# A decoder layer's attention: the softmax denominators summed from a GpSimd pre-addition, after the value passes

## What is computed

```python
scores = jnp.einsum('bhsd,bhtd->bhst', q, k)
scores = (scores + alibi[None]) / math.sqrt(D_HEAD)
scores = 30.0 * jnp.tanh(scores / 30.0)
scores = jnp.where(causal[None, None], scores, -jnp.inf)
probs = jax.nn.softmax(scores, axis=-1)
ctx = jnp.einsum('bhst,bhtd->bhsd', probs, v)
ctx = ctx.transpose(0, 2, 1, 3).reshape(N, S, N_HEADS * D_HEAD)
return ctx @ Wo + bo
```

## Time and profile before

| | us |
|---|---|
| median of 3 runs | 1212.09 (1209.39 to 1213.41) |
| span of the profiled execution, first to last instruction | 1209.9 |
| its own time | not listed apart from the three runs above |
| TensorE busy | 1179.2 (97% of the span) |
| VectorE / GpSimd / ScalarE busy | 862.2 / 583.5 / 531.2 |

### The profile page before, as it was taken

One profiled execution on the slowest core, in us unless ns is written; L12 is line 12 of the kernel. 1 busy time (PEld: TensorE's weight loads), 2 busy tenths in 40 slices (PEclk: granted clock), 3 DMA queues, 4 the chain that ended last, 5 costly groups with the idle time before them and its releaser, 6 DMA issues.

```text
span 1209.9 us, 24907 instructions
## 1 busy us (share of the span) xinstructions
PE 1179.2 (97%) x9875; PEld 816.0 (67%) x9890; DVE 862.2 (71%) x1286; ACT 531.2 (44%) x598; POOL 583.5 (48%) x493
## 2 busy tenths in 40 slices
PE   4989999999999999999999999999999999999998
PEld 3656557656657566576565677777886786786784
DVE  6787978777877777688787588889653653654554
ACT  6676664654655645637556400000342432432341
POOL 0445454644645546445456399998332322322221
PEclk9989999999999999999999999999999999999999
DMA  9463352544335425434355367771000000000000
GB/s 325 136 199 117 118 160 70 161 157 118 116 126 169 132 89 168 162 103 131 108 170 168 128 129 151 147 143 50 1 1 18 1 19 18 0 17 18 1 18 35
DMA packets 128126, 124.04 MB, mean 103 GB/s; under 512 B 31612, under 2 KB 89346, under 8 KB 128066
## 3 DMA queue, kind: packets, MB, share of 16 engines
q1 hardware_dynamic: 103112, 117.00, 31.6%
q10 hardware_dynamic: 24960, 6.29, 3.2%
HBM read 81.76 MB, written 35.21 MB: 97 GB/s over the span
## 4 chain that ended last, share of the span: by engine, by line
PE 89%; DVE 4%; ACT 2%; DMA 2%; POOL 1%; issue 1%; SPq 1%; POOLq 0%; DVEq 0%; ACTq 0%
PE bank L885 12%; PE bank L641 11%; PE bank L642 10%; PE bank L643 10%; PE bank L961 9%; PE bank L962 9%; PE bank L717 6%; PE bank L984 5%; PE bank L983 4%; PE bank L706 3%; PE bank L707 3%; PE bank L719 3%; DMA unit_halves<-halves 1%; PE bank L649 1%; ACT region_c L1098 1%
## 5 line engine op out<-in xcount | busy, mean ns | idle before, releaser
L1877 POOL TENSOR_TENSOR parts<-parts 128x512 f32<-128x512 f32 x80 | 130.3, 1632 | 118.0 <-DVE parts L1353 118.0
L641 PE MATMUL bank<-hT_hi,w_hi 128*128 128x256 f16 x640 | 175.7, 274 | 4.8 <-DVE hT_lo L1337 4.8
L642 PE MATMUL bank<-hT_lo,w_hi 128*128 128x256 f16 x640 | 175.4, 274 | 0.0
L643 PE MATMUL bank<-hT_hi,w_lo 128*128 128x256 f16 x640 | 175.3, 274 | 0.0
L1882 POOL TENSOR_SCALAR_AFFINE_SELECT region_c<-region_c 128x512 f32<-128x512 f32 x128 | 106.9, 859 | 135.6 <-ACT region_c L1101 135.5
L885 PE MATMUL bank<-kv,toep 128*128 128x288 f32 (+2 forms) x660 | 157.8, 401 | 0.7 <-ACT qT L1134 0.5
L885 PEld LDWEIGHTS bank<-kv,toep 128*128 128x128 f32 x660 | 123.7, 190 | 34.0 <-ACT qT L1134 0.7
L1098 ACT ACTIVATE region_c<-bank,cap_scale 128x1536 f32<-128x1536 f32 x64 | 98.7, 1542 | 94.2 <-PE bank L707 93.7
L1888 POOL TENSOR_TENSOR ctx_lo<-ctx,ctx_hi 128x512 f16<-128x512 f32 x64 | 89.0, 1392 | 83.4 <-ACT ctx_hi L1077 83.4
L2011 POOL TENSOR_TENSOR sqsum<-sqsum,toep 128x512 f32<-128x512 f32 x56 | 71.1, 1269 | 110.1 <-ACT toep L1263 110.0
L961 PE MATMUL bank<-odd_hi,guT 128*128 128x256 f16 x512 | 112.4, 273 | 0.0
(11 more groups left out here) (177 smaller groups left out, 2638.6 us busy)
## 6 DMA issues: line engine op xcount, KB each, us to landing
unit_halves<-halves SPq DMA_DIRECT2D x80, 256.0 KB, 2.2
q_both<-unit_halves SPq DMA_DIRECT2D x64, 256.0 KB, 2.9
q_high<-unit_halves SPq DMA_DIRECT2D x64, 128.0 KB, 3.0
toep<-kernel_padded SPq DMA_DIRECT2D x32, 256.0 KB, 4.1
wffn<-w_gu SPq DMA_DIRECT2D x6, 1280.0 KB, 6.2
cpair<-ctx_pairs SPq DMA_DIRECT2D x32, 176.0 KB, 4.7
xin<-x SPq DMA_DIRECT2D x8, 512.0 KB, 3.7
region_o<-wq SPq DMA_DIRECT2D x4, 1024.0 KB, 11.2
```

The source lines that it names most:

```text
L641: pe.matmul(dst, lh, rh, start=first and k == 0, stop=False)
L642: pe.matmul(dst, lh, rl, start=False, stop=False)
L643: mm = pe.matmul(dst, ll, rh, start=False, stop=last and k == n - 1)
L1877: pool.tensor_tensor(slot[:, 0], slot[:, 0], slot[:, 1], ALU.add).then_inc(unit_summed, 1)
```

## The change

GpSimd gets one more instruction per group, behind the two mask selects: it adds the second key tile's masked weights to the first tile's, for queries 128 to 255, into a new buffer of two slots. The sums become two sets of four 128-column products with ones: queries 0 to 127 from the first tile, queries 128 to 255 from the new buffer. They stand behind the two value passes, and wait for the addition. The addition waits for the masks, and from group 2 on for the sums of two groups before. ScalarE's wait for group 5's slot is now on the sums. `gsum` goes, to make room, and the thresholds' sums are kept in `gthr`.

```diff
--- before.py
+++ after.py
@@ -166,9 +166,9 @@
             dist_scale = sb1("dist_scale", [P, Q_PIECES])
             undo_o = sb1("undo_o", [P, 1])
             dcol = sb1("dcol", [HM, 1])
-            gsum = sb1("gsum", [P, WQT, 512 // GROUP])
+            gthr = sb1("gthr", [P, WQT, 512 // GROUP])
             gscale = sb1("gscale", [P, WQT, 512 // GROUP], BF16)
-            gthr = sb1("gthr", [P, WQT, 512 // GROUP])
+            key_sum = sb1("key_sum", [P, 2, REP, P])
 
             w_bf = sb1("w_bf", [P, WQT, 512], BF16)
             wffn = sb1("wffn", [P, WQT, 512])
@@ -316,6 +316,7 @@
         tanh_done = sem("tanh_done")
         exp_done = sem("exp_done")
         masked = sem("masked")
+        keys_added = sem("keys_added")
         pv_filled = sem("pv_filled")
         sums_filled = sem("sums_filled")
         rsum_turned = sem("rsum_turned")
@@ -724,9 +725,6 @@
                 if g == 0 and first:
                     pe.wait_ge(unit_turned, 6)
                     pe.wait_ge(wscale_step, SCALE_STEPS * I_Q[3] + 1)
-                if g or not first:
-                    pe.wait_ge(rsum_turned, NG * b + g)
-                weigh(bank[:, SUM_BANK, 0:S], g % 3, lambda t: sum_ones[:]).then_inc(sums_filled, 1)
                 if g == 0:
                     pe.wait_ge(v_ready, TT * (b + 1))
                 if g >= 2 or not first:
@@ -734,6 +732,14 @@
                 for v in range(2):
                     mm = weigh(bank[:, pv_bank(g), v * S:(v + 1) * S], g % 3, lambda t: value_half(t, g, v))
                 mm.then_inc(pv_filled, 1)
+                pe.wait_ge(keys_added, NG * b + g + 1)
+                if g or not first:
+                    pe.wait_ge(rsum_turned, NG * b + g)
+                for j in range(REP):
+                    mm = pe.matmul(bank[j * SQ:(j + 1) * SQ, SUM_BANK, 0:P], sum_ones[:], sc_first[:, g % 3, j, 0:P], start=True, stop=True)
+                for j in range(REP):
+                    mm = pe.matmul(bank[j * SQ:(j + 1) * SQ, SUM_BANK, P:S], sum_ones[:], key_sum[:, g % 2, j, :], start=True, stop=True)
+                mm.then_inc(sums_filled, 1)
 
             def output(b, g):
                 pe.wait_ge(ctx_lo_done, NG * b + g + 1)
@@ -1117,7 +1123,7 @@
                         high_unit(b, EARLY + step - 2)
                     if step == NG:
                         round_share(b)
-                act.wait_ge(pv_filled, NG * b + LAST_IN_CUT + 1)
+                act.wait_ge(sums_filled, NG * b + LAST_IN_CUT + 1)
                 for tiles in HALVES:
                     spread(b, gthr, w_cut, THRESHOLDS, tiles)
                 high_ctx(b, NG - 1, False)
@@ -1461,10 +1467,10 @@
             def find_thresholds(f):
                 base = QUANT_STEPS * f
                 dve.wait_ge(w_rounded, f + 1)
-                dve.tensor_reduce(gsum[:], w_bf[:].rearrange("p t (n c) -> p t n c", c=GROUP), AX_X, ALU.add,
+                dve.tensor_reduce(gthr[:], w_bf[:].rearrange("p t (n c) -> p t n c", c=GROUP), AX_X, ALU.add,
                                   apply_absolute_value=True).then_inc(quant_step, 1)
                 dve.wait_ge(quant_step, base + 1)
-                dve.tensor_scalar(gscale[:], gsum[:], 1.0 / GROUP, 1e-8, ALU.mult, ALU.max).then_inc(quant_step, 1)
+                dve.tensor_scalar(gscale[:], gthr[:], 1.0 / GROUP, 1e-8, ALU.mult, ALU.max).then_inc(quant_step, 1)
                 dve.wait_ge(quant_step, base + 2)
                 dve.tensor_scalar(gthr[:], gscale[:], 257.0 / 512.0, None, ALU.mult).then_inc(quant_step, 1)
                 dve.wait_ge(quant_step, base + 3)
@@ -1882,6 +1888,11 @@
                     last = pool.affine_select(s, s, pattern=[[0, REP], [1, P]],
                                               compare_op=ALU.is_ge, fill=0.0, base=0, channel_multiplier=-1)
                 last.then_inc(masked, 1)
+                n = NG * b + g + 1
+                pool.wait_ge(masked, n)
+                if g >= 2:
+                    pool.wait_ge(sums_filled, n - 2)
+                pool.tensor_tensor(key_sum[:, g % 2], sc_first[:, g % 3, :, P:S], sc_second[:, g % 3], ALU.add).then_inc(keys_added, 1)
 
             def low_ctx(b, g):
                 pool.wait_ge(ctx_hi_done, NG * b + g + 1)
```

## The result

The changed kernel takes **1234.34 us** (median of 4, 1232.58 to 1235.86) against 1212.59 of the kernel before (4 runs, 1209.39 to 1213.41): ratio **1.0181 [1.0168, 1.0194]**, slower by some 22 us. The forecast was 1227.3, in a range to 1236.

What follows compares the result with a forecast made beforehand. TensorE, 89% of the chain, was taken as the bound. Six loop batches of +2.5 us made +15.2, the ends -0.4 and +0.4: span 1209.9 to 1225.1, by the median 1227.3; range 1206 to 1236.

Steps and rivals of the forecast that it cites:

- Removed: In TensorE's sums, two 128-column halves take 0.22 instead of 0.45 us: 0.22 less a group, 1.76 a batch.
- That the halves don't save: Rival: the two 128-column halves take no less, as the second needs a switch; +14 on top, chance 0.02.
- The addition: One GpSimd addition of 128x512 float32 per group, behind the masks: 1.25 us plus 0.1 for its wait.
- The cheap addition: Rival: the GpSimd addition takes 0.6 us like a select; -6, 1206, faster, chance 0.12.
- Place 1: Step 7, next batch's normalisation: addition between mask and deviation, turn 1.35 later, TensorE waits 2 us; net +0.03 a batch.
- Place 3, output(0): Step 5: additions delay masks, parts and low_ctx(0), which ends about 323.1; TensorE waits about 0.9 us.
- Place 2, output(1): Step 6: VectorE's wide addition gets in before low_ctx(1), which output(1) needs; TensorE waits about 1.6 us.
- The exclusion: A VectorE instruction with two SBUF inputs and a GpSimd one reading SBUF exclude each other for the whole instruction.
- Only Place 1 counts: Rival: no wait at output(0) and (1), as VectorE's wide work finds another gap; -2, 1210, chance 0.16.
- The clock falls: Rival: TensorE's clock falls behind the turn's wait, from 1.3 us more idle time on; +29, 1241, chance 0.07.
- The ends: First batch -0.4 (bounds -1.8 and +1.8); last batch +0.4, from -1.8, +1.6 at output(1) and +0.6 at output(3).
- Costed at nothing (a): VectorE's chain of a group starts some 1.3 us later, behind the value passes; nothing, or 1.3 a batch if cover failed.

Runs made afterwards that it cites:

- experiment 3: Changed kernel without the addition, second half of the sums reading the second key tile alone, exponential's scale 0.01 instead of 30: 1204.37 us, 0.9936.
- experiment 6: Changed kernel with each addition one step later, before the next masks, and the deviation ahead of mask(7), in the last batch of mask(5): 1202.94 us, 0.9929.
- experiment 10: Kernel before with only the deviation ahead of mask(7) in the loop and of mask(5) in the last batch: 1211.0 us, 0.9991.
- experiment 4: Changed kernel with keep_x2 and the deviation ahead of addition 7 in step 7 of the loop: 1225.58 us, 1.0107.
- experiment 7: Changed kernel with VectorE's 3584-wide subtraction of step 4 cut to 8 elements: 1234.54 us, 1.0186.
- experiment 1: Changed kernel with the old sums (256 + 128 columns) and no addition, value passes still ahead of the sums: 1213.61 us, 1.0013.
- experiment 2: Changed kernel with its addition and waits, but the old sums of 256 + 128 columns: 1231.08 us, 1.0149.
- experiment 9: Changed kernel with every addition done twice in a row: 1299.23 us, 1.0736.
- experiment 5: Changed kernel with each addition one step later in GpSimd's queue, ahead of the next group's masks: 1213.34 us, 1.0013.
- experiment 11: Kernel of experiment 6 with the old sums in the old order and no additions in the first and last batch: 1201.14 us, 0.9912.

## Why the prediction was right, and where not

The forecast, slower, held, and in the main by its mechanism: the additions' places in GpSimd's queue cost more than the shorter sums give. A third of the loss (6.8 of 21.3) is the falling clock, which it had as a rival. By its own steps:

- **Removed.** 0.22 a group was 0.21, 1.70 a batch (experiment 3, and 6 against 10). That the halves don't save, a rival, falls.
- **The addition.** 1.25 + 0.1: median 1.277, and masks to power grew by 1.35. Near VectorE's work it took up to 2.93. The cheap addition, a rival, falls.
- **Place 1.** Right: 1.99 before the turn, and all of a batch's saving lost in it. Experiments 4 to 6 show that two things hold it, not only the queue: whatever GpSimd does while VectorE standardises x delays x. The prediction didn't say that.
- **Place 3, output(0).** 0.9 was 0.43: the place was right, the chain through masks, parts and additions ended some 0.5 earlier than my count (batch 3 runs 6.44 later than on the old axis; low_ctx(0) ends at 328.97, so at 322.5 and not 323.1).
- **Place 2, output(1).** 1.6 was 0.95. **This is the failed step**: "TensorE arrives at 328.90 - 4 x 0.22 = 328.0" leaves out the wait that Place 3 had just put in front of it. mask(4) hangs on scores(4), which come before output(0); a wait at output(0) delays TensorE and not GpSimd. I used this for the later outputs, but not here. The rest of the count was right: on the old axis the wide addition ended at 328.5, as forecast, and low_ctx(1) at 329.5 for 329.7, but TensorE came at 328.6. With my own 0.9 the wait would have been 0.7, and the sum 1.6 a batch where 1.69 was measured. The listed waits explain 0.43 + 0.95 + 0.07 = 1.45 of it. The rest is in the starts: against experiment 6's loop batch, which has no waits, output(0) starts 0.50 late, output(1) 1.02 more and the turn 2.06 more, each 0.07 above its listed wait, and output(2) 0.09 more. These 3.67, less the 0.30 that the turn cost before (experiment 10) and the 1.71 saved, are 1.66.
- **The exclusion.** It decided Place 2: low_ctx(1) took 2.93 us beside the wide addition and 1.16 without it (experiment 7). The Trainium skill (SBUF — State Buffer, "Who interferes with whom") says that a VectorE instruction with two SBUF inputs contends with a GpSimd one that reads SBUF. The traces agree. What I got wrong is only what follows, in experiment 7's forecast: taking the meeting away moved the wait on.
- **Only Place 1 counts**, a rival at 0.16: falls, the outputs wait twice in each batch.
- **The clock falls**, a rival at 0.07: **it happened, in 4 of 6 batches**. Its size was right (2 us a fall; 1.7), the point from which it should decide was not: it was said to need 1.3 us more idle time than 2 us, from a single case of 3.3. The row itself says otherwise: TensorE had stopped at 72.8, and a mean clock of 0.73 from 74 to 76 puts the fall at 74.9, 2.1 us after that.
- **The ends.** First batch -0.4 was +1.6. The order alone, costed at nothing, came with 2.2 there (experiment 1), and not by the chain that "Costed at nothing (a)" names: ScalarE waited longer for Wo. As the first turn differs by 1.7 between two kernels with the same batch 0 (experiment 7 and the changed kernel), the sizes of its parts stay open. Last batch +0.4 was +2.7: sums 0.40, output(0) 1.46, output(1) 1.02 and output(3) 1.24, 4.1 of waits against 1.7 saved. I had two of these four.

So the 1227.3 came close partly by luck, by errors that cancelled: 5.1 too much in the loop (15.2 for 10.1), against 6.8 of clock, 2.0 and 2.3 for the ends, 11.1 too little: 6.0 short in the spans, 7.0 in the medians. The upper end of the range, 1236, stood for an addition of 1.5 us; the addition took 1.277, and it was the clock that brought the time near that end.

## What to carry over

An instruction on an engine that is half idle costs by its place in the queue: put it where that engine waits for its input anyway (before the next group's masks, not behind this group's), and this change turns from +22 to +1 us; with the deviation moved ahead as well it is -9, and with the old sums in the two end batches -11. Waits aren't additive: each one gives the other engines time, so the next is to be counted from an arrival that includes it, and one removed may come back one output later. Work saved on the bounding engine before a fixed wait becomes idle time, and idle time there can cost the clock on top.

## What the runs showed of the hardware

- TensorE's granted clock fell from 1.00 to 0.50 behind an idle stretch of 2.0 us in four of six batches, at the same place with the same work in front of it, and in three of six in experiment 7; behind 1.56 us in none of six (experiment 2). With every addition twice (experiment 9) it fell behind 2.65 us in one of three batches, behind 3.33 in three of three, before output(0), behind 3.45, in three of six, and before output(1), behind 2.18, in the other three of these. In the long convolution it fell beside a wait of 0.43 us in six of the thirteen profiled executions (experiments 2, 4, 5, 7, 10 and 11), and cost 1.0 to 1.4 us there. So from 0.43 to 3.45 us of idle time it fell in some places and not in others: the length of the wait alone doesn't decide it, and what does is not settled by these runs. A fall in the loop cost 1.7 us, and 2 us of useless products kept it away.
- A GpSimd addition and VectorE's standardising of x also hold each other up, though x has one tensor as its input beside two numbers per row: two tiles took 2.79 us beside an addition and a low part (experiments 4 and 5) and 1.84 beside a low part alone (344.64 to 345.80) in the kernel before. The median over all single tiles of the kernel before is 0.54.
